# Order of the first integers on VectorE and of the gate scales on GpSimd in a gated cross-attention and quantised feed-forward kernel

## The reference

```python
def _act_fake_quant(x, clip_factor):
    scale = jax.nn.sigmoid(clip_factor) * jnp.max(jnp.abs(x)) / QMAX
    return jnp.clip(_ste_round(x / scale), -QMAX - 1.0, QMAX) * scale
...
xq = _act_fake_quant(x, clip_x[0])
gate = jnp.einsum('bsh,ih->bsi', xq, _weight_fake_quant(w_gate))
up = jnp.einsum('bsh,ih->bsi', xq, _weight_fake_quant(w_up))
h = _act_fake_quant(jax.nn.silu(gate) * up, clip_down[0])
return jnp.einsum('bsi,hi->bsh', h, _weight_fake_quant(w_down))
...
x = x + jnp.tanh(g_xattn[0]) * _L0_xattn_ref(_layernorm(x, axis=-1), ctx_1024, ctx_1024, L0_xattn_Wq, L0_xattn_Wk, L0_xattn_Wv)
x = x + jnp.tanh(g_ffn[0]) * _L0_ffn_ref(_layernorm(x, axis=-1), L0_ffn_clip_x, L0_ffn_clip_down, L0_ffn_w_gate, L0_ffn_w_up, L0_ffn_w_down)
```

## Time and profile before

| | |
|---|---|
| median of 3 runs | 112.05 us (112.00 to 112.37) |
| the profiled execution's own time | 111.74 us |
| its span in the profile | 109.9 us |
| TensorE busy | 100.7 us (92%) |
| VectorE busy | 84.6 us (77%) |
| ScalarE busy | 67.8 us (62%) |
| GpSimd busy | 51.6 us (47%) |

### The profile page before, as it was taken

How to read it: one execution, slowest core, us unless ns; L and a number is a source line. 1 busy time by engine, 2 the same in 40 slices (tenths; PEclk the granted TensorE clock), 3 DMA queues, 4 the chain that set the end, 5 groups by cost and what they waited for, 6 DMA issues and landing times.

```text
span 109.9 us, 1783 instructions
## 1 busy us (share of the span) xinstructions
PE 100.7 (92%) x590; PEld 76.7 (70%) x592; DVE 84.6 (77%) x208; ACT 67.8 (62%) x128; POOL 51.6 (47%) x86
## 2 busy tenths in 40 slices
PE   5899999999999999999999975999998899799960
PEld 2278888888888898888898952444443598577740
DVE  0366294797998798868589978749999997899992
ACT  0421262369863746568579975888988761999300
POOL 7224053073553708161390790076668622599900
PEclk9999999999999999999999999999999999999999
DMA  3999999997000000000000000000000000015555
GB/s 37 384 380 261 397 421 425 407 410 313 12 0 0 3 0 6 0 3 0 0 0 0 0 0 0 6 3 0 0 0 0 0 6 0 0 36 192 175 180 188
DMA packets 5513, 11.65 MB, mean 106 GB/s; under 512 B 640, under 2 KB 2688, under 8 KB 5504
## 3 DMA queue, kind: packets, MB, share of 16 engines
q1 hardware_dynamic: 4928, 10.75, 26.7%
q10 hardware_dynamic: 576, 0.79, 2.1%
HBM read 9.44 MB, written 2.10 MB: 105 GB/s over the span
## 4 chain that ended last, share of the span: by engine, by line
PE 51%; DVE 34%; issue 6%; ACT 4%; DMA 3%; DVEq 0%
PE ps L463 13%; PE ps L485 11%; PE ps L511 10%; DVE hmax L1108 8%; DVE shared L1103 5%; DVE ps L1140 4%; DVE xs L1144 4%; DMA wq_sb<-in_wq 3%; PE ps L521 2%; PE ps L523 2%; PE ps L522 2%; PE ps L665 2%; PE ps L568 2%; ACT silu L851 2%; PE ps L495 2%
## 5 line engine op out<-in xcount | busy, mean ns | idle before, releaser
L665 PE MATMUL ps<-xq,wguT 128*128 128x512 bf16 x78 | 17.6, 379 | 1.6 <-DVE xq L1084 1.6
L425 POOL TENSOR_TENSOR shared<-up_sb,silu 128x1024 f32<-128x1024 f32 x5 | 11.8, 2366 | 10.6 <-ACT up_sb L856 10.6
L665 PEld LDWEIGHTS ps<-xq,wguT 128*128 128x128 bf16 x80 | 7.5, 97 | 11.4 <-DVE shared L1103 1.1
L463 PE MATMUL ps<-wvT,shared 128*128 128x256 f32 x56 | 13.3, 380 | 0.0
L485 PE MATMUL ps<-shared,a_sb 128*128 128x256 f32 x56 | 13.2, 379 | 0.0
L851 ACT ACTIVATE silu<-ps,gu_scale 128x1024 f32<-128x1024 f32 x10 | 11.1, 1114 | 3.3 <-PE ps L665 3.3
L1108 DVE TENSOR_REDUCE hmax<-shared 128x1 f32<-128x2048 f32 (+1 forms) x6 | 12.6, 2108 | 0.6
L371 POOL TENSOR_SCALAR var<-mv 128x2 f32<-128x2 f32 x8 | 1.5, 192 | 22.7 <-DVE mv L947 22.5
L511 PE MATMUL ps<-uT,shared 128*128 128x256 f32 (+1 forms) x64 | 11.9, 329 | 0.0
L463 PEld LDWEIGHTS ps<-wvT,shared 128*128 128x128 f32 x56 | 10.6, 190 | 1.7 <-DMA shared<-in_xc 0.3
L711 PE MATMUL ps<-wdT,hq 128*128 128x256 bf16 x80 | 11.0, 273 | 0.6 <-DVE hq L1155 0.5
(11 more groups left out here) (139 smaller groups left out, 212.7 us busy)
## 6 DMA issues: line engine op xcount, KB each, us to landing
shared<-in_xc SPq DMA_DIRECT2D x6, 512.0 KB, 10.6
out<-xs SPq DMA_DIRECT2D x7, 256.0 KB, 2.2
xs<-in_x SPq DMA_DIRECT2D x3, 512.0 KB, 8.4
shared<-in_wgu SPq DMA_DIRECT2D x3, 512.0 KB, 7.9
shared<-in_xc SPq DMA_DIRECT2D x4, 256.0 KB, 5.9
wd<-in_wd SPq DMA_DIRECT2D x1, 768.0 KB, 11.6
wq_sb<-in_wq ACTq DMA_DIRECT2D x1, 256.0 KB, 3.7
wk_sb<-in_wk SPq DMA_DIRECT2D x1, 256.0 KB, 3.6
```

Of the source, the lines that this page charges most:

```text
L425: nc.gpsimd.tensor_tensor(hid[:, 2 * i + 1, :], up_sb[i % 2][:], silu1[i % 2][:], ALU.mult).then_inc(hid_done[1], 1)
L463: last = nc.tensor.matmul(bank2(VB[b])[:, k, :], ctxT(b)[:, e, k * P:(k + 1) * P], weights[:, e, :], start=(e == 0), stop=(e == KT - 1))
L665: last = nc.tensor.matmul(bank(4 * half + 2 * g + c), wguT[:, i, g, k, :], xq[:, k, col:col + CH], start=(k == 0), stop=(k == KT - 1))
```

## The change

On GpSimd the scaling of `gu_scale` moves behind the conversion of batches 4 and 5. On VectorE the conversion of batch 2 moves ahead of the two clips of chunk 0. No instruction is added or taken away, and each keeps its operands and its waits.

```diff
-            pool.wait_ge(act_scale_done, 1)
-            nc.gpsimd.tensor_scalar(gu_scale[:].rearrange("p s n -> p (s n)"), wscale[:].rearrange("p s n -> p (s n)"),
-                                    act_scale[:, 0:1], 1.0, ALU.mult, ALU.mult).then_inc(gu_scale_done, 1)
-
             pool.wait_ge(act_inv_done, 1)
             pool.wait_ge(xn2T_ready, 2)
             nc.gpsimd.tensor_scalar(xq_i16[:, :, 2 * CH:3 * CH], xn2T[:], act_inv[:, 0:1], 1.0, ALU.mult,
                                     ALU.mult).then_inc(xq_int_pool, 1)
+            pool.wait_ge(act_scale_done, 1)
+            nc.gpsimd.tensor_scalar(gu_scale[:].rearrange("p s n -> p (s n)"), wscale[:].rearrange("p s n -> p (s n)"),
+                                    act_scale[:, 0:1], 1.0, ALU.mult, ALU.mult).then_inc(gu_scale_done, 1)
...
             dve.wait_ge(act_inv_done, 1)
-            for c, b in enumerate((0, 2)):
+            for b in (0, 2):
                 input_ints(b)
+            for c in range(2):
                 dve.wait_ge(xq_int_dve, c + 1)
                 dve.wait_ge(xq_int_act, c + 1)
                 for k in range(KT):
```

## The result

The changed kernel took 111.43 us (median of 7 runs, 111.26 to 111.84) against 112.10 us before (7 runs, 112.00 to 112.43). The ratio is 0.9931 with a 95% interval of 0.9913 to 0.9949, so it is 0.7% faster, 0.67 us by the medians. The forecast was 111.4 us and a gain of 0.66 us.

What follows compares the result with a forecast made beforehand. The prediction took the bound to be VectorE's first clip waiting for GpSimd's conversion, delaying TensorE's third gate matmul. Moving that matmul from 67.43 to 66.77 gains 0.66 us: 112.05 − 0.66 = 111.39, rounded to 111.4 us, range 111.0 to 111.9.

Steps and rivals of the forecast that it cites:

- The reading of the long first clip as a wait for GpSimd's conversion: VectorE's first clip, recorded at 0.87 us against 0.27 for the second: some 0.60 us are waiting for GpSimd's SBUF access.
- The sign that the prediction took from one row: At the stalled first clip on VectorE: it ends 0.14 us behind the recorded end of GpSimd's conversion.
- The prediction had the third matmul move by 0.66 us: TensorE's third gate matmul starts at 66.77 instead of 67.43, its clip being ready at 66.60.
- the hold by the gate scales that the prediction allowed for: VectorE's first clip, possible at 65.91, starts at 65.92, when the hold by GpSimd's gate scales ends.
- The signs that the prediction named: Behind the inverse's end: GpSimd's conversion 0.2 us, first clip about 1.4, third gate matmul 2.27, product(1) 8.24.
- The rival in which VectorE's two PSUM conversions hold up GpSimd's: GpSimd's conversion waits until 65.95, the third matmul comes 0.36 us later than now: 112.4 us; chance 0.08.
- feared up to 0.28 us from the gate scales: GpSimd's gate scales between the clips of chunks 0 and 1 cost at most 0.28 us, leaving a gain of 0.38.
- the prediction's case of late gate scales: Gate scales behind all clips end at 67.77, first silu at about 67.9; largest value ends near 71.4; no cost.
- The gap of 0.41 us: Unexplained "issue" on VectorE between the silu of slot 1 and product(1); taken to move along with the gain.
- The rival in which the gap closes: The gap ahead of product(1) shrinks to 0.13 us, gain 1.01 us, down to 111.04; chance 0.04.
- what starts product(1) earlier starts the rest earlier by as much: Behind product(1) VectorE is full, so the gain carries on whole up to the second barrier and beyond.
- The rule on the shared ports: VectorE and GpSimd lock the SBUF ports per instruction; to the letter, first clip held until 66.05, gain 0.53 us.

Runs made afterwards that it cites:

- act45_before: The kernel before, with the conversion of batches 4 and 5 moved from GpSimd to ScalarE, VectorE's order old; 111.47 us, ratio 0.9954.
- double_conv: The changed kernel, with GpSimd's conversion of batches 4 and 5 done once more ahead of the real one; 112.34 us, ratio 1.0032.
- vec_only: VectorE's new order alone, with GpSimd's old order, against the kernel before; 111.53 us, ratio 0.9941.
- pool_only: GpSimd's new order alone, with VectorE's old order, against the kernel before; 111.90 us, ratio 0.9979.
- split2: The changed kernel, with the second feature half of batch 2 converted by ScalarE behind batch 3; 111.29 us, ratio 0.9931 to the kernel before.
- gu_late: The changed kernel, with the gate scales held until all six clips are done; 111.34 us, ratio 0.9933 to the kernel before.
- swap_waits: The changed kernel, with VectorE's two waits ahead of each product swapped, silu first, then up; 110.98 us, ratio 0.9897 to the kernel before.
- pad8: The changed kernel plus eight one-column writes to an unused tile behind VectorE's last clip; 111.12 us, ratio 0.9903 to the kernel before.
- small_first: The changed kernel, with GpSimd's product of slot 0 cut from 1024 to 64 columns; 111.36 us, ratio 0.9945 to the kernel before.

## Why the prediction was right

**What bounds the stretch.** The reading of the long first clip as a wait for GpSimd's conversion is shown from both sides. Without that conversion the clip takes 0.29 us (act45_before), and with two of them 1.18 us (double_conv). The sign that the prediction took from one row, that the clip ends 0.14 us behind GpSimd's recorded end, returned as 0.14 or 0.15 in vec_only, pool_only, split2 and double_conv.

**VectorE's part.** The conversion of batch 2 fills the wait at no cost: both PSUM conversions took 0.75 and 0.74 us beside a running GpSimd. The prediction had the third matmul move by 0.66 us; it moved by 0.71, from 2.90 to 2.19 behind the mark. The 0.05 lie in the first clip, which the prediction let end where it did before, 1.66 us behind the mark; it ended at 1.61. Only 0.01 of that is the hold by the gate scales that the prediction allowed for (65.91 to 65.92). Nearly all the rest is VectorE's own step: the clip started 0.66 us behind the conversion ahead of it, where the prediction had 0.70 (65.21 to 65.91) and gave no row for it.

The signs that the prediction named are there, counted from the end of the inverse (64.84): GpSimd's conversion starts at 0.17, the first clip at 1.35, the third matmul at 2.21 and product(1) at 8.16. The rival in which VectorE's two PSUM conversions hold up GpSimd's is out: that conversion took 1.12 us beside both, as before.

**GpSimd's part.** The prediction took its effect on the clips as nothing, and feared up to 0.28 us from the gate scales. Nothing is right: the clips did not wait. The meeting cost 0.15 us on the gate scales, and gu_late shows that these can end over a microsecond later for free. One sum in the prediction's case of late gate scales is off: with product(0) at about 69.1 the largest value ends near 71.6, not 71.4. It is still over a microsecond ahead of product(1), so nothing hangs on it. What the part brings is 0.06 us in the new order (vec_only 8.20, changed 8.14) and 0.24 in the old one (pool_only).

**The way to the end.** Product(1) moved by 0.73 us and the end by 0.72. The gap of 0.41 us moved along, as assumed. It was an assumption, though, and the largest open term. That the timed gain of 0.67 us meets the forecast of 0.66 so closely is partly luck: the profile says 0.72, and the interval of the ratio runs from 0.57 to 0.98 us. The rival in which the gap closes was worth 1.01 us in the prediction, with all of it reaching the end. In swap_waits and pad8 it did close, and only 0.33 or 0.34 us of some 0.4 reached the end. The step "what starts product(1) earlier starts the rest earlier by as much" holds up to about 0.33 us below the changed kernel's 8.14. Beyond it the largest value of slot 1 waits for GpSimd's product.

**The rule on the shared ports.** Taken to the letter it would have given 0.53 us at the third matmul; measured are 0.71. The Trainium skill, "SBUF — State Buffer", section "SBUF: two separate sides", has an exclusive lock that whoever starts first holds for the whole instruction. The runs agree with the exclusion (1.18 us in double_conv). But a start in the record is not yet the hold. In pool_only and split2 the gate scales are recorded while a clip still waits, and in the changed kernel 0.08 us ahead of a new one; each time they are the ones that grow, to 0.43 us. In double_conv GpSimd's second conversion is recorded ahead of the clip by the same 0.083 us as the gate scales in the changed kernel, and there the clip waits. The recorded starts don't decide who goes on, and no run shows what does.

**What stays open** is what makes the 0.41 us. It is not GpSimd's product (small_first). In the changed kernel they lie behind a separate wait of the sequencer that is released by the silu. Such a wait alone costs 0.04 us (product(0), and product(1) in pad8), so some 0.37 us belong to something else. With eight more instructions ahead they are gone, and the instruction load on queue 14 has moved away as well. That speaks for a dependence on the place in VectorE's program. swap_waits fits it: the place and the load stay, but the separate wait ends 0.52 us before the silu, which is enough to hide 0.41. The load itself starts behind product(1), so at most it marks the place and is not what the product waited for. What happens at that place no run shows.

## What to carry to other kernels

An instruction that is much longer than its twins next to it may have a wait inside, as here, and the place to look for its cause is the end of whatever runs beside it. Such a wait can be filled with work that doesn't need the contended resource (here a conversion from PSUM) as well as removed. Count from a mark in front of the change, not from the start of the span: here the two profiles differed by 0.33 us before the change had begun, half of the effect. A gap that no row explains is worth one cheap trial of moving what stands around it; here that was another 0.33 us in the profile, and for free. The instruction loads in the DMA view are worth a look at such a gap.

## What the runs showed of the hardware that was not expected

- Of two engines that meet, the one recorded first is not always the one that goes on. In the changed kernel a VectorE clip starting 0.083 us behind GpSimd's recorded start of the gate scales took its plain 0.28 us and stretched the GpSimd instruction from 0.28 to 0.43 us. In double_conv a clip starting the same 0.083 us behind a conversion was the one that waited, 1.18 us.
- A gap of 0.41 us ahead of one instruction shrank to 0.04 when eight instructions of 0.17 us in all were added at an idle place ahead of it. An instruction load of 8192 bytes, which in the twelve other profiles starts 0.55 to 0.95 us behind that instruction, then came 5.12 us ahead of it. The last instruction of VectorE came 0.34 us earlier in the profile (41.73 against 42.07 us behind the mark); in the timed runs the ratios to the kernel before are 0.9903 and 0.9931, and their intervals overlap.
